# Where VectorE's sums of token chunks stand at the end of a mixture-of-experts stage: among its last three turns, or all behind them

## The chip, the cores and the metric

One core of one Trainium2 chip runs the whole program in one launch. The metric is the device time of that launch in microseconds (us). TensorE (PE), VectorE (DVE), ScalarE (ACT) and GpSimd (POOL) each run their own instruction stream in order; SyncE (SP) does no arithmetic here and issues most of the DMAs. The streams are tied together by semaphores.

## The reference

The input is 16 batches of 256 tokens with 128 features, so 4096 tokens. A causal attention layer with a graph part comes first, then a mixture of experts:

```python
x = x + _L0_attn_ref(_layernorm(x, axis=-1), ...)      # 16 heads of 64, causal
x = x + _L0_ffn_ref(_layernorm(x, axis=-1), ...)
# _L0_ffn_ref: 8 experts, hidden size 352, every token goes to its top 2 experts
normed = _rmsnorm(x, norm_weight)
probs = softmax(normed @ router_weight.T); topk_w, topk_idx = top_k(probs, 2)
for e in range(E):
    hidden = silu(gate) * up
    moe_out = moe_out + combine[..., e, None] * (hidden @ down_weight[e].T)
return x + alpha * moe_out
```

What this study is about is the very last line. Each token's result is its own row plus the two rows that its two experts gave.

## The kernel before

The kernel has a long attention part (one turn for each batch, two batches written out, then a hardware loop) that ends at about 880 us. After it comes the sorted stage. Every token has been copied twice, once for each of its two experts, into a DRAM tensor `slots` in which the copies are sorted by expert and cut into tiles of 128 rows. There are 71 such tiles (`STEPS` = 71), and one step works on one of them:

- SP loads the tile into `zin` (a ring of 8), L436.
- PE transposes it, multiplies it with the expert's gate and up weights (`sorted_gate_up`, L1009), transposes the hidden rows (`hidden_transposed`, L1020) and multiplies them with the down weights into bank 7 (`sorted_down`, L1042).
- ACT takes the high part of the transposed tokens, the silu and the transposed hidden rows out of PSUM. DVE takes the low part (`slots_low`, L1966) and the product of silu and up (`sorted_hidden`, L1971). It then scales the down product out of bank 7 into `zout` (`slots_out`, L1979 to L1984).
- POOL scatters the 128 rows of `zout` into the DRAM tensor `pairs` with an indirect DMA (`rows_out`, L565 to L570). Its landing raises `w_row[j % 8]`.

The steps are software-pipelined. Turn j of DVE's loop runs `sorted_hidden(j)`, `slots_low(j + 2)` and `slots_out(j - 2)`, and the loop has 73 turns (0 to 72). Turn 70 is the last with a `sorted_hidden`; turns 71 and 72 hold only `slots_out(69)` and `slots_out(70)`.

In `pairs` both rows of a token lie side by side. The output is made in 8 chunks of 512 tokens (`CHUNK` = 4 tiles of 128). `fetch(k)` reads chunk k of `pairs` into `got`, 512 KB, and raises `w_got[k]`. Then three rows are added: `x_all`, `got[.., 0, :]` and `got[.., 1, :]`. The chunks are shared out:

- `BY_DVE` = chunks 0, 1, 2 and 6, in two tensor_tensor operations each (`total`, L2019 to L2023). The second one raises `d_sum`.
- `BY_PE` = chunks 3, 4 and 5, by multiplying with the identity and adding up in PSUM (L1112 to L1119), from where ACT copies them back (L1358 to L1361) and raises `a_sum`.
- Chunk 7, `FINAL`, is halved: 256 tokens by DVE, 256 by PE and ACT.

Chunks 0 to 6 hold the batches 0 to 13 and chunk 7 the batches 14 and 15. Rows of the early batches are all out once the first `DONE` steps have landed, so the first seven chunks are fetched before the last steps are through. `FINAL` needs all 71 steps.

SP's stream sets the order of the transfers at the end (L451 to L465). SP works through it in order, and a wait holds everything behind it:

```python
            all_rows(DONE)
            for k in range(CHUNKS_DONE):
                fetch(k)
            for n in range(3):
                store(chunk(BY_DVE[n]), d_sum, n + 1)
            store(chunk(BY_PE[0]), a_sum, 1)
            all_rows(STEPS)
            fetch(FINAL)
            store(chunk(BY_DVE[3]), d_sum, 4)
```

`store(t, by, n)` (L424 to L426) waits until `by` has reached n and then writes 256 KB of `x_all` to the output (128 KB for the halves of chunk 7). `all_rows` (L428 to L430) is eight waits, one for each `w_row`.

Of the kernel before, what the change touches and what calls it, by code (L numbers as in the profile page):

```python
# [36 lines left out]
STEPS = BATCHES * SIDE + EXPERTS - 1  # L37
# [41 lines left out]
def build_program(nc, x, wq, wk, wv, wvT, gnn_w, gnn_b, lin_wT, lin_b, wo, gamma_in, gamma_out,  # L79
# [10 lines left out]
    with ctx:  # L90
# [252 lines left out]
        def live(j):  # L343
            return 0 <= j < STEPS
# [3 lines left out]
            return (j - slot + RING - 1) // RING  # L348

        BY_PE, BY_DVE, FINAL = (3, 4, 5), (0, 1, 2, 6), CHUNKS_OUT - 1  # L350
        AMONG_STEPS = {STEPS - 1: 0, STEPS: 1, STEPS + 1: 2}
        FINAL_PE = slice(FINAL * CHUNK, FINAL * CHUNK + CHUNK // 2)
        FINAL_DVE = slice(FINAL * CHUNK + CHUNK // 2, CHUNKS_OUT * CHUNK)

        def chunk(k):
            return slice(k * CHUNK, (k + 1) * CHUNK)
# [1012 lines left out]
        def _(dve):  # L1369
# [126 lines left out]
            def output_bias(b):  # L1496
                s_og.wait(dve, b, PAIRS)
                V.tensor_scalar(yT[:, :], bank[7][:, 0:TOKENS], yb[:, :], None, ALU.add).then_inc(d_yT.sem, 1)

            def output_kept(b, o):  # L1500
                s_yn.wait(dve, b, 1)
                V.tensor_copy(y_now[:, :, :],  # L1502
                              o.rearrange("p (t d) -> p t d", t=TILES)).then_inc(d_y.sem, 1)
# [462 lines left out]
            def slots_low(j):  # L1966
                a_zh.wait(dve, j, 1)
                V.scalar_tensor_tensor(sz_lo[:, j % 2, :], bank[4][:, 0:P], normw[:, :],
                                       sz_hi[:, j % 2, :].bitcast(f32), ALU.mult, ALU.subtract).then_inc(d_zlo.sem, 1)

            def sorted_hidden(j):  # L1971
                s_gu.wait(dve, 2 * j, 2)
                a_silu.wait(dve, j, 1)
                if j >= 2:
                    s_ht.wait(dve, j - 2, 1)
                V.tensor_tensor(shid[:, j % 2, 0:HID], bank[2 + j % 2][:, 0:HID], ssg[:, j % 2, :],  # L1976
                                ALU.mult).then_inc(d_hid.sem, 1)

            def slots_out(j):  # L1979
                s_down.wait(dve, j, 1)  # L1980
                if j >= RING:
                    dve.wait_ge(w_row[j % RING], 16 * (j // RING))
                V.tensor_scalar(zout[:, j % RING, :], bank[7][:, 0:DIM], zin[:, j % RING, SHARE:SHARE + 1], None,  # L1983
                                ALU.mult).then_inc(d_zout.sem, 1)  # L1984
# [5 lines left out]
            def taken_from_bank(k):  # L1990

                p, last = BATCHES - 2, BATCHES - 1
                if k == 0:
                    take_logits(p, bank[7][:, AUX_LOGITS])
                if k == 4:
                    take_places(p, bank[7][:, AUX_PLACES])
                if k == 19:
                    last_transposed(bank[7][:, AUX_Z])
                if k == 21:
                    take_logits(last, bank[7][:, AUX_LOGITS])  # L2000
                if k == 25:
                    take_places(last, bank[7][:, AUX_PLACES])

            def routed(j):
                p, last = BATCHES - 2, BATCHES - 1
                if 2 <= j < 6:
                    choose(p, (0, 'index', 'hot', 2)[j - 2])
                if 6 <= j < 8:
                    place_tokens(p, j - 6)
                if 8 <= j < 20:  # L2010
                    norm_tokens(last, j - 8)
                if 23 <= j < 27:
                    choose(last, (0, 'index', 'hot', 2)[j - 23])
                if 27 <= j < 29:
                    place_tokens(last, j - 27)
                if 29 <= j < 37:
                    table_rest(j - 29)

            def total(t, k, n):  # L2019
                dve.wait_ge(w_got[k], 16)  # L2020
                V.tensor_tensor(got[:, t, 0, :], got[:, t, 0, :], got[:, t, 1, :], ALU.add).then_inc(d_part, 1)
                dve.wait_ge(d_part, n + 1)
                V.tensor_tensor(x_all[:, t, :], x_all[:, t, :], got[:, t, 0, :], ALU.add).then_inc(d_sum, 1)  # L2023

            def sorted_stage():
                V.memset(shid[:, :, HID:], 0.0)
                slots_low(0)
                output_bias(BATCHES - 1)
                slots_low(1)
                for j in range(STEPS + 2):  # L2030
                    if live(j):
                        sorted_hidden(j)
                    if live(j + 2):
                        slots_low(j + 2)
                    if j == 1:
                        output_kept(BATCHES - 1, bank[7][:, 0:TOKENS])
                    if live(j - 2):
                        s_down.wait(dve, j - 2, 1)
                        taken_from_bank(j - 2)
                        slots_out(j - 2)  # L2040
                    routed(j)
                    if j in AMONG_STEPS:
                        n = AMONG_STEPS[j]
                        total(chunk(BY_DVE[n]), BY_DVE[n], n)

            dve.wait_ge(w_x0, 16)
            norm_step(0, 0)
# [15 lines left out]
            with dve.Fori(2, BATCHES - 1) as b:  # L2063
                batch(b, b - 1, b - 2, b + 1)
            batch(BATCHES - 1, BATCHES - 2, BATCHES - 3, None)
            sorted_stage()
            total(chunk(BY_DVE[3]), BY_DVE[3], 3)
            total(FINAL_DVE, FINAL, len(BY_DVE))


# [22 lines left out]
```

## Time and profile before

| | before |
|---|---|
| median of 3 runs | 1054.04 us (1053.72 to 1056.16) |
| the profiled execution, device time | 1054.87 us |
| its span in the trace | 1053.1 us |
| PE / DVE / ACT / POOL busy | 97% / 81% / 74% / 48% of the span |
| granted TensorE clock, mean | 1.0 |
| got<-pairs, 8 fetches of 512 KB | 6.0 us median from issue to landing |
| out<-x_all, 7 stores of 256 KB | 3.5 us median from issue to landing |

All times in the trace count from the start of the span. The busy shares are means over the whole program; the change touches only the last 17 us. Of DMA issues, "issue" is the moment when the engine hands the transfer over, and "landing" is when the semaphore that it raises is complete.

### The profile page before, as it was taken

Reading aid. Unit: us, or ns where it says so; the run is one execution under the profiler, and the core shown is the slowest. Engines: PE = TensorE matmul, PEld = TensorE weight load, DVE = VectorE, ACT = ScalarE, POOL = GpSimd, SP = SyncE. Lnnn points to the kernel's source line nnn. Section 1 sums busy time; section 2 is a strip of 40 time slices with the busy share of each in tenths; the row PEclk is TensorE's granted clock in tenths of the full one; section 3 lists DMA queues with packets and bytes.
Section 4 is the critical chain, followed back from the end, with each engine's and each line's share of the span. In section 5 each row is a group of like instructions: output and inputs, shape, how many; then the busy total and the mean of one; then the engine's idle time right before and its main releaser. Section 6 shows DMA issues by size and latency. Waiting matters only on the chain.

```text
span 1053.1 us, 27818 instructions
## 1 busy us (share of the span) xinstructions
PE 1022.9 (97%) x8600; PEld 855.3 (81%) x8600; DVE 856.3 (81%) x3622; ACT 777.8 (74%) x2180; POOL 505.3 (48%) x668
## 2 busy tenths in 40 slices
PE   4999999999999999999999999999999999999997
PEld 3888888887888888888887878888887877999995
DVE  4859798989898988889898989898989787767554
ACT  3778787878787878787878787878787785656663
POOL 4524345454545454545454545454545352655443
PEclk9999999999999999999999999999999999999999
DMA  6990000000000000000000000000000022222227
GB/s 176 401 358 15 1 10 12 8 10 8 10 8 10 8 10 8 10 8 10 8 10 8 10 8 10 8 8 11 8 11 5 6 68 54 74 62 72 60 66 249
DMA packets 48965, 50.04 MB, mean 48 GB/s; under 512 B 20601, under 2 KB 39291, under 8 KB 48912
## 3 DMA queue, kind: packets, MB, share of 16 engines
q1 hardware_dynamic: 44592, 40.91, 12.7%
q0 software_dynamic: 4320, 8.47, 2.4%
q8 instruction: 28, 0.46, 0.2%
q14 instruction: 25, 0.20, 0.1%
HBM read 21.23 MB, written 28.58 MB: 47 GB/s over the span
## 4 chain that ended last, share of the span: by engine, by line
PE 78%; DVE 11%; ACT 3%; issue 3%; DMA 2%; SPq 2%; POOL 0%; POOLq 0%; DVEq 0%; ACTq 0%
PE bank L665 65%; DVE eb L1475 4%; DVE ea L1472 3%; PE bank L742 2%; PE bank L752 2%; PE bank L1025 2%; PE bank L753 2%; PE bank L755 2%; DVE nmax L1462 2%; PE bank L777 2%; ACT ea L1159 1%; ACT eb L1159 1%; DMA pairs<-zout,zin 1%; PE bank L1007 1%; DVE y_now L1502 1%
## 5 line engine op out<-in xcount | busy, mean ns | idle before, releaser
L535 POOL TENSOR_TENSOR ea<-ea,wgt 128x256 f32<-128x256 f32 x128 | 79.9, 624 | 273.1 <-DVE wgt L1484 273.0
L1462 DVE TENSOR_REDUCE nmax<-bank 128x1 f32<-128x128 f32 (+1 forms) x512 | 149.7, 347 | 22.3 <-PE bank L665 21.6
L1475 DVE SCALAR_TENSOR_TENSOR eb<-idw,ssum,eb 128x256 f32<-128x256 f32 x256 | 136.9, 570 | 0.0
L537 POOL TENSOR_TENSOR eb<-eb,wgt 128x512 f32<-128x512 f32 x128 | 133.9, 1046 | 0.0
L1159 ACT ACTIVATE eb<-bank,nmax 128x256 f32<-128x256 f32 x256 | 126.8, 495 | 0.0
L1129 ACT ACTIVATE gt<-bank 128x512 f32<-128x512 f32 (+1 forms) x256 | 112.7, 499 | 15.1 <-PE bank L755 12.9
L1159 ACT ACTIVATE ea<-bank,nmax 128x128 f32<-128x128 f32 x256 | 98.4, 385 | 27.1 <-DVE nmax L1462 22.3
L665 PE MATMUL bank<-qk 64*128 64x128 f32 (+1 forms) x1024 | 111.0, 341 | 0.0
L568 POOL DMA_INDIRECT pairs<-zout,zin x71 | 70.8, 997 | 78.7 <-DVE zout L1983 67.2
L665 PE MATMUL bank<-gt,vnat 128*64 128x256 f32 (+1 forms) x1024 | 107.2, 335 | 0.4 <-ACT gt L1129 0.4
L665 PE MATMUL bank<-gt,g 128*64 128x256 f32 (+1 forms) x1024 | 92.2, 327 | 0.3 <-ACT g L1129 0.3
L665 PEld LDWEIGHTS bank<-gt,vnat 128*64 128x64 f32 x1024 | 63.2, 136 | 35.6 <-issue 16.0
L1129 ACT ACTIVATE gvT<-bank 128x256 f32<-128x256 f32 x128 | 49.9, 390 | 55.8 <-DVE aT L1494 55.7
L1472 DVE SCALAR_TENSOR_TENSOR ea<-ident,ssum,ea 128x128 f32<-128x128 f32 x256 | 90.9, 391 | 0.0
L1129 ACT ACTIVATE qk<-bank 128x512 f32<-128x512 f32 x128 | 76.1, 610 | 19.6 <-PE bank L665 18.1
L665 PE MATMUL bank<-xt_lo,w_hi 128*128 128x256 f32 x256 | 87.3, 341 | 2.4 <-DVE xt_lo L1455 1.7
L544 POOL TENSOR_TENSOR deg<-den,rs 128x256 f32<-128x256 f32 x128 | 81.6, 642 | 12.9 <-DVE eb L1475 12.9
L665 PEld LDWEIGHTS bank<-gt,g 128*64 128x64 f32 x1024 | 65.4, 137 | 21.0 <-ACT g L1129 0.7
L665 PE MATMUL bank<-f2T,lwo 128*128 128x256 f32 x256 | 77.7, 386 | 0.3 <-ACT f2T L1192 0.3
L1976 DVE TENSOR_TENSOR shid<-bank,ssg 128x352 f32<-128x352 f32 x71 | 37.2, 524 | 50.1 <-ACT ssg L1322 38.2
L665 PE MATMUL bank<-aT,wo_sb 128*128 128x256 f32 x256 | 73.7, 391 | 0.0
L665 PE MATMUL bank<-xt_hi,w_hi 128*128 128x256 f32 x256 | 72.5, 283 | 0.0
(241 smaller groups left out, 3007.2 us busy)
## 6 DMA issues: line engine op xcount, KB each, us to landing
slots<-gu_lo SPq DMA_DIRECT2D x33, 520.0 KB, 15.0
zin<-slots SPq DMA_DIRECT2D x71, 65.0 KB, 1.9
got<-pairs SPq DMA_DIRECT2D x8, 512.0 KB, 6.0
zin<-in_guT SPq DMA_DIRECT2D x14, 216.0 KB, 2.8
raw_gu<-in_guT SPq DMA_DIRECT2D x8, 352.0 KB, 3.0
out<-x_all SPq DMA_DIRECT2D x7, 256.0 KB, 3.5
pairs<-zout,zin POOLq DMA_INDIRECT x71, 2.3
dn<-in_downT SPq DMA_DIRECT2D x2, 512.0 KB, 15.7
```

What stands on the lines that cost most here:

```text
L535: nc.gpsimd.tensor_tensor(ea[:, s], ea[:, s], wgt[:, s, 0:2].unsqueeze(2).to_broadcast([P, 2, P]), ALU.mult)
L537: nc.gpsimd.tensor_tensor(eb[:, s], eb[:, s], wgt[:, s, 2:4].unsqueeze(2).to_broadcast([P, 2, 2 * P]), ALU.mult).then_inc(p_g.sem, 1)
L544: nc.gpsimd.tensor_tensor(deg[:, s], den[:, s, :].unsqueeze(2).to_broadcast([P, 4, DHEAD]), rs[:, s, :].unsqueeze(2).to_broadcast([P, 4, D ...
L568: nc.gpsimd.indirect_dma_start(pairs, bass.IndirectOffsetOnAxis(ap=zin[:, j % RING, ID:ID + 1].bitcast(u32), axis=0), zout[:, j % RING, :] ...
L665: return nc_mm(o, st, mo, start=first, stop=last, **more)
L742: mm = nc.tensor.transpose(o[:, m * TOKENS + t * P:m * TOKENS + (t + 1) * P], vnat[:, t, n * P:(n + 1) * P], ident[:, :])
L1129: return nc.scalar.activation(o, i, ACT.Copy, **more)
L1159: done = nc.scalar.activation(e[:, s, a, :], score_bank(n, a)[:, TILE_SCORES[t]], ACT.Exp, bias=nmax[:, s, i:i + 1], accum_out=ssum[:, s, ...
L1462: done = V.tensor_reduce(nmax[:, n % 3, i:i + 1], score_bank(n, a)[:, TILE_SCORES[t]], X, ALU.max, negate=True)
L1472: V.scalar_tensor_tensor(ea[:, s, a, :], ident[:, :], ssum[:, s, a:a + 1], ea[:, s, a, :], ALU.mult, ALU.max, accum_out=den[:, s, a:a + 1])
L1475: done = V.scalar_tensor_tensor(eb[:, s, a, :], idw[:, :], ssum[:, s, 2 + a:3 + a], eb[:, s, a, :], ALU.mult, ALU.max, accum_out=den[:, s, ...
L1976: V.tensor_tensor(shid[:, j % 2, 0:HID], bank[2 + j % 2][:, 0:HID], ssg[:, j % 2, :], ALU.mult).then_inc(d_hid.sem, 1)
```

## The change

The three sums that stood in DVE's turns 70, 71 and 72 (behind `slots_out(68)`, `slots_out(69)` and `slots_out(70)`) are taken out of the loop. The four whole chunks are now summed one after the other behind the last turn, in the same order and with the same semaphore counts. Nothing else differs: not SP's stream, not PE's, ACT's or POOL's.

```diff
         BY_PE, BY_DVE, FINAL = (3, 4, 5), (0, 1, 2, 6), CHUNKS_OUT - 1
-        AMONG_STEPS = {STEPS - 1: 0, STEPS: 1, STEPS + 1: 2}
...
                     routed(j)
-                    if j in AMONG_STEPS:
-                        n = AMONG_STEPS[j]
-                        total(chunk(BY_DVE[n]), BY_DVE[n], n)
...
             sorted_stage()
-            total(chunk(BY_DVE[3]), BY_DVE[3], 3)
+            for n, k in enumerate(BY_DVE):
+                total(chunk(k), k, n)
             total(FINAL_DVE, FINAL, len(BY_DVE))
```

## Rows read from the trace of the kernel before

**Rows 1.** Chain that ended last, 1035 to 1054: start us, us, what.
```profile
1035.98 0.36 DVE zout L1983
...
1039.03 1.22 POOL pairs L568
...
1040.96 3.21 DMA pairs<-zout,zin
...
1044.64 4.14 DMA got<-pairs
...
1048.83 1.58 PE bank L665 x6
...
1050.42 0.38 ACT x_all L1129
```

**Rows 2.** Timeline of DVE: start us, us, operation, idle before and its releaser.
```profile
1036.97 0.69 DVE L2023 TENSOR_TENSOR x_all<-x_all,got 128x512 f32<-128x512 f32 x1
1037.91 0.35 DVE L1983 TENSOR_SCALAR zout<-bank,zin 128x128 f32<-128x128 f32 x1 [0.25 <-PE bank L665]
...
1039.83 0.35 DVE L1983 TENSOR_SCALAR zout<-bank,zin 128x128 f32<-128x128 f32 x1 [0.25 <-PE bank L665]
1040.10 0.68 DVE L2021 TENSOR_TENSOR got<-got 128x512 f32<-128x512 f32 x1
1040.82 0.69 DVE L2023 TENSOR_TENSOR x_all<-x_all,got 128x512 f32<-128x512 f32 x1
1041.42 0.68 DVE L2021 TENSOR_TENSOR got<-got 128x512 f32<-128x512 f32 x1
1042.14 0.69 DVE L2023 TENSOR_TENSOR x_all<-x_all,got 128x512 f32<-128x512 f32 x1
1048.80 0.43 DVE L2021 TENSOR_TENSOR got<-got 128x256 f32<-128x256 f32 x1 [5.97 <-DMA got<-pairs]
```

**Rows 3.** Timeline of SP's DMA issues, single ones, same columns.
```profile
1027.93 0.33 SPq L436 DMA_DIRECT2D zin<-slots  x1
...
1028.57 0.33 SPq L422 DMA_DIRECT2D got<-pairs  x1
...
1041.53 0.45 SPq L426 DMA_DIRECT2D out<-x_all  x1
1042.97 0.37 SPq L426 DMA_DIRECT2D out<-x_all  x1
1044.64 0.34 SPq L422 DMA_DIRECT2D got<-pairs  x1
1045.04 0.43 SPq L426 DMA_DIRECT2D out<-x_all  x1
1050.83 0.37 SPq L426 DMA_DIRECT2D out<-x_all  x1
```

**Rows 4.** Timeline of ACT, its first copy of a chunk's sum.
```profile
1042.35 0.60 ACT L1129 ACTIVATE x_all<-bank 128x512 f32<-128x512 f32 x1 [3.68 <-PE bank L665]
```

**Rows 5.** Tile view of x_all on SP, 1042 to 1044: one store, issue to landing.
```profile
L426 SPq DMA_DIRECT2D out<-x_all x1: 372/372/372, 1043.0 to 1043.0; - x1
...
DMA to landing us min/median/max: 2.3/2.3/2.3
```

**Rows 6.** DMA view of 1043 to 1044 in 40 slices, busy tenths.
```profile
DMA  9999999999989999995531111011000000034789
```

**Rows 7.** Tile view of got on SP, seventh fetch alone: issue to landing.
```profile
L422 SPq DMA_DIRECT2D got<-pairs x1: 486/486/486, 1031.5 to 1031.5; - x1
...
DMA to landing us min/median/max: 9.0/9.0/9.0
```

**Rows 8.** Timeline of POOL, scatters of steps 67, 69 and 70.
```profile
1035.03 0.97 POOL L568 DMA_INDIRECT pairs<-zout,zin  x1 [1.01 <-DVE zout L1983]
...
1039.03 1.40 POOL L568 DMA_INDIRECT pairs<-zout,zin  x1 [0.53 <-issue]
1040.96 1.40 POOL L568 DMA_INDIRECT pairs<-zout,zin  x1 [0.53 <-issue]
```

**Rows 9.** Windows of half a microsecond: PE, PEld, DVE, ACT, POOL, clock, DMA share, GB/s.
```profile
1047.50:1048.00 0.50, 0.00 (x0) 0.00 (x0) 0.00 (x0) 0.50 (x1) 0.00 (x0) 1.00 0.97 373
...
1048.50:1049.00 0.50, 0.17 (x1) 0.18 (x2) 0.20 (x1) 0.00 (x0) 0.00 (x0) 1.00 1.15 345
```

## The prediction

> **What bounds the kernel now.** The page says that TensorE is busy for 97% of the span, but the change touches nothing before 1036 us, so that share says nothing about it. I read the chain of work that ended last, and of it only the end [rows 1]. The reader is to see which waits are in it. Up to 1035.98 it is TensorE. Then it goes through DVE's `zout` and POOL's scatters to the last scatter, issued at 1040.96 and landed 3.21 us later, at about 1044.2. From there it goes to SP's fetch of the last chunk at 1044.64, which lands 4.14 us later. PE's last sum (1.58 us), ACT's copy (0.38) and the last store, issued at 1050.83 [rows 3], end the program. None of DVE's sums of whole chunks is in the chain. Two questions are left. Do the sums hold up the `zout`s that are in it? And does the fetch stay where it is when the stores ahead of it on SP come later?
>
> **What the change removes: the sums among the turns.** DVE's timeline answers the first question [rows 2]. The first sum ends at 1036.97 + 0.69 = 1037.66, and the `zout` behind it starts at 1037.91 after 0.25 us of idle time that PE ended. The next one is the same (idle 0.25, ended by PE). So both `zout`s wait for PE's down product and not for a sum; taking the sums away moves neither. Value 0 us. Bounds: no gain above 0, because PE's product is late by itself, and no loss, because nothing is added in front of them.
>
> On POOL the same scatter takes 0.97 us at 1035.03 and 1.40 at 1039.03 and 1040.96 [rows 8]; the 0.43 us come with the sums, as each long one overlaps a second addition of a sum (1040.82 to 1041.51 for the last [rows 2]). After the change the scatters of steps 68 and 69 have no sum beside them and should fall to 0.97. The last one should not: the first sum now starts where the third one did, at 1040.10, right behind the last `zout`, and its second addition again runs from 1040.82 to 1041.51. The last scatter is the one the fetch needs, so 0 us are won.
>
> The Trainium skill's page "SBUF — State Buffer", section "SBUF: two separate sides", says that a VectorE instruction with two SBUF inputs excludes a GpSimd instruction that reads SBUF. The rows above agree (+0.43 us), and by that rule too the last scatter stays at 1.40.
>
> **What it adds: three sums behind the turns.** DVE has four sums to make in a row. From one sum's first addition to the next one's it is 1041.42 - 1040.10 = 1.32 us [rows 2]. The sums then start at 1040.10, 1041.42, 1042.74 and 1044.06, and end 1.41 later (1040.82 + 0.69 - 1040.10): 1041.51, 1042.83, 1044.15 and 1045.47. The fourth one was done at 1042.14 + 0.69 = 1042.83 and is now 2.64 us later. DVE's half of the last chunk starts only at 1048.80 after 5.97 us of idle time [rows 2], which covers that; without this cover it would cost the 2.64.
>
> **What waits for the later sums: SP.** This is the only term that isn't zero. SP issues the three stores of DVE's chunks, PE's first store, eight waits, and then the last fetch, strictly in this order. Before, the third store was issued at 1041.53, PE's first at 1042.97 (released by ACT's copy, 1042.35 + 0.60 [rows 4]), and the fetch at 1044.64 (released by the last scatter) [rows 3]. So SP stood still from 1043.34 until 1044.2, which is cover for a delay. After:
>
> - the third store follows its sum: 1044.15 + 0.02 = 1044.17 (before: 1041.53 after 1041.51)
> - PE's first store has long been ready and follows after one issue of 0.45: 1044.62, and takes 0.37: 1044.99
> - eight waits that are all met: 0.31, from the end of the load before (1027.93 + 0.33 = 1028.26) to 1028.57 [rows 3]
> - the fetch is issued at 1045.30 instead of 1044.64: +0.66 us.
>
> Of 2.64 us of delay about 2.0 are hidden by the time SP stood waiting, first for ACT and then for the last scatter. The last scatter has landed by 1044.2, so its landing no longer sets the fetch; the third sum does.
>
> **What lies in front of the fetch in the DMA engines.** The second cost is unseen in the trace and I bound it. A lone store of 256 KB lands in 2.3 us [rows 5]. The DMA view around it shows the previous store's packets until about 1043.5 and its own from about 1043.9, 0.93 us after its issue at 1042.97 [rows 6]. It was issued 1.44 us after the store before it, whose packets would by the same lag start near 1042.46 and end near 1043.45; so one store keeps the engines busy for an estimated 0.97 us. Before, both stores' packets were through by 1044.9, ahead of the fetch's (1044.64 + 0.93 = 1045.57). After, the third store's packets start at 1045.10 and end at 1046.07, PE's first store's end at 1047.04, and the fetch could start at 1045.30 + 0.93 = 1046.23. If the engines take it in strict order it starts at 1047.04, 0.81 us later still. If its reads overlap with the stores, nothing is added. Lower bound 0, upper bound 0.81. I take 0.4, the middle: a store writes DRAM and a fetch reads it, and no row here has a fetch behind two stores, so neither end is nearer.
>
> The Trainium skill's page "DMA: Bandwidth & Descriptors", section "Queues, rings and completion order", says that descriptors of one queue are consumed in ring order on each DMA engine. No row here tests it; by this rule the cost would be the full 0.81, and the total +1.47 instead of +1.06.
>
> **The sum.** 0.66 + 0.4 = +1.06 us for the landing of the last chunk: 1048.78 becomes about 1049.84. What follows it (PE 1.58, ACT 0.38, the last store) is unchanged: PE's other sums are done at 1047.5 in both. So the span goes from 1053.1 to 1054.2 us. The profiled execution's own time was 1054.87, 1.77 above its span and 0.83 above the median of the runs. On the median the forecast is 1054.04 + 1.06 = 1055.1 us, +0.1%. That is below the 0.3% (3.2 us) that a measurement of this kernel can tell from no change, so the forecast is "no difference", leaning to slower.
>
> **The rivals.**
>
> (a) *The last fetch is caught in a pile of transfers: slower.* In the trace, a fetch landed after 4.14 us when it was nearly alone [rows 1], but the seventh of seven in a row took 9.0 [rows 7]. After the change up to three stores (issued at 1042.85, 1044.17 and 1044.62) are not yet through when the fetch is handed over. If they count like fetches, the fetch takes up to 9.0: +4.86, and with the 0.66 the end is +5.5, 1059.6 us. It decides from a landing of more than 4.14 + 2.5 = 6.6 us on. Against it: the six fetches in front of the seventh were 3 MB, three stores are 0.75 MB. Chance 4%.
>
> (b) *TensorE's clock falls while PE waits for the last chunk.* PE now idles from 1047.5 to about 1049.9 instead of 1048.8. The granted clock is 1.00 in the idle stretch and behind it [rows 9]. If the longer wait brought it to the lower of the two levels (1.2 instead of 2.4 GHz), PE's last sum of 1.58 would take up to twice that: +1.58 on +1.06, 1056.7 us. Nothing in the trace shows such a fall, so 5%, and it too stays within 0.3%.
>
> (c) *The scatters get faster and the fetch earlier: a gain.* The last scatter landed 3.21 us after its issue [rows 1], while the second and third stores of DVE's chunks were under way. If it lost the 0.43 us of contention [rows 8] and SP were ready, the fetch would come at 1044.2: -0.43, 1053.6 us. For this SP would have to be through with the third store by 1043.4, but the third sum ends at 1044.15. Chance 8%, for the case that DVE's four sums run closer together than the 1.32 us read here or that the fetch lands faster behind later stores.
>
> (d) *The change does nothing of what it says.* The order is written out by hand and nothing reorders it, so this has no chance worth a number.
>
> **How the numbers follow.** The forecast (+0.66 to +1.47) has 80%, (a) 4%, (b) 5%, (c) 8%, and 3% are left for something unseen, split over both sides. For 8 in 10 the range runs from the median less (c)'s 0.43 and the spread of the runs' lower side (0.3), 1053.3, up to (b)'s 1056.7 with 0.3 on top, 1057.0; it leaves out (a). By the 0.3% bound: faster 2% (half of the unseen rest), within 93%, slower 5% ((a) and the other half).
>
> **What would show each step.** `zout` at 1037.9 and 1039.8 as before, both still released by PE; the scatters of steps 68 and 69 at 0.97 us and the last at 1.40; four sums in a row, 1.32 apart from 1040.1 on; SP's third store at 1044.2, the fetch at 1045.3; a landing of 4.1 to 5.0 us. In the chain of work, SP's stores and DVE's sums should take the place of the last scatter. The prediction is wrong if the `zout`s come earlier without the sums, if the fetch is issued outside 1045.0 to 1045.6, or if its landing takes over 6.6 us.

## The result and the profile after

| | before | after the change |
|---|---|---|
| median of 22 runs each | 1054.78 us (1053.72 to 1057.39) | 1056.92 us (1055.61 to 1058.45) |
| ratio to before, 95% interval | | 1.0018 (1.0012 to 1.0024) |
| profiled execution: device time, span | 1054.87, 1053.1 us | 1056.03, 1054.3 us |

The change costs 2.1 us by the medians (+0.2%), twice what was forecast. It is clear of zero but within the 0.3% that count as no difference here. The forecast started from a median of 3 runs, 1054.04 us; with 22 runs the kernel before stands at 1054.78.

The two profiled executions differ by only 1.2 us. In the one of after, the last `zout` starts at 1039.06 and not at 1039.83 [rows 2]. This lead is older than the change: the `zout` of step 68, ahead of the first sum that was moved, starts at 1035.21, where it was 1035.98 before [rows 1]. So from here on most times are counted **from the start of the last `zout`**, written +x. Counted so, before ends at 1053.1 - 1039.83 = +13.27 and after at 1054.3 - 1039.06 = +15.24. The difference is 1.97 us, close to the 2.14 of the medians.

The chain of work that ended last, after the change (start us, us, what), against [rows 1]:

```profile
1039.06 0.35 DVE zout L1982
1039.41 0.61 DVE got L2020
...
1042.69 0.70 DVE x_all L2022
1043.40 0.02 issue
1043.41 0.37 SPq L425
1043.79 0.05 issue
1043.84 0.50 SPq L425
1044.34 0.05 issue
1044.38 0.02 SPq L429
...
1044.52 0.03 SPq L429
1044.55 0.35 issue
1044.90 0.03 SPq L429
1044.93 0.05 issue
1044.98 4.37 DMA got<-pairs
...
1049.39 2.25 PE bank L664 x6
...
1051.66 0.38 ACT x_all L1128
```

POOL's scatter, which linked the last `zout` to the fetch before, is gone from the chain. In its place stand three sums of DVE, two stores on SP and SP's waits (the eight waits show as four rows of L429). The row of 0.35 us between two of them is called "issue" in the trace: SP waits for nothing there that the profile shows. It is called a pause below. PE's last sum takes 2.25 us where it took 1.58.

POOL's timeline after, against [rows 8], the scatters of steps 69 and 70:

```profile
1038.26 0.97 POOL L567 DMA_INDIRECT pairs<-zout,zin  x1 [0.95 <-DVE zout L1982]
1040.18 1.40 POOL L567 DMA_INDIRECT pairs<-zout,zin  x1 [0.96 <-DVE zout L1982]
```

The last scatter is still beside a sum, the one ahead of it is free of it. DVE's timeline after has the last `zout`, against [rows 2], still released by PE:

```profile
1039.06 0.35 DVE L1982 TENSOR_SCALAR zout<-bank,zin 128x128 f32<-128x128 f32 x1 [1.57 <-PE bank L664]
```

And windows of half a microsecond (columns as in [rows 9]):

```profile
1049.50:1050.00 0.50, 0.50 (x3) 0.45 (x4) 0.47 (x2) 0.00 (x0) 0.00 (x0) 1.00 1.15 345
1050.00:1050.50 0.50, 0.50 (x3) 0.45 (x2) 0.25 (x1) 0.00 (x0) 0.00 (x0) 0.63 1.07 322
1050.50:1051.00 0.50, 0.50 (x3) 0.34 (x1) 0.00 (x0) 0.00 (x0) 0.00 (x0) 0.50 0.49 147
```

The third column from the right is the granted clock. It goes from 1.00 (2.4 GHz) to 0.50 (1.2 GHz) in the middle of PE's last sum, after PE had nothing to do for 2.71 us. Before, PE idled 1.36 us there and the clock stayed at 1.00 [rows 9].

### The profile page after: what moved, and what is told of

Read it like the earlier page. It is cut to its first block, busy times and chain, and to the rows that moved or that the text cites. A ratio compares the mean times of both kernels' runs of the same rounds, so it can differ in the third digit from the quotient of the medians.

```text
span 1054.3 us, 27818 instructions
## 1 busy us (share of the span) xinstructions
PE 1023.3 (97%) x8600; PEld 855.6 (81%) x8600; DVE 856.2 (81%) x3622; ACT 776.9 (74%) x2180; POOL 503.5 (48%) x668
## 4 chain that ended last, share of the span: by engine, by line
PE 79%; DVE 12%; ACT 3%; issue 3%; SPq 2%; DMA 2%; DVEq 0%; POOLq 0%; ACTq 0%
PE bank L664 65%; DVE eb L1474 4%; DVE ea L1471 3%; PE bank L741 2%; PE bank L751 2%; PE bank L1024 2%; PE bank L754 2%; PE bank L752 2%; DVE nmax L1461 2%; PE bank L776 2%; ACT eb L1158 1%; ACT ea L1158 1%; PE bank L1006 1%; DVE y_now L1501 1%; DVE yT L1497 1%
## 5 line engine op out<-in xcount | busy, mean ns | idle before, releaser
L536 POOL TENSOR_TENSOR eb<-eb,wgt 128x512 f32<-128x512 f32 x128 | 133.6, 1044 | 0.0
```

Source lines behind the costliest of these rows:

```text
L536: nc.gpsimd.tensor_tensor(eb[:, s], eb[:, s], wgt[:, s, 2:4].unsqueeze(2).to_broadcast([P, 2, 2 * P]), ALU.mult).then_inc(p_g.sem, 1)
```

## The experiments

All were run with the kernel before beside them. The values below are from the profiled executions, in us from the last `zout`; the last two columns are from all runs (5 to 22 a kernel). One kernel has one profile, so differences of 0.1 or 0.2 us between two rows of the other columns may be chance. "Lands in" is the time from issue to landing of the last fetch, taken from the chain or, where the fetch isn't in it, from DVE's first work on the chunk.

| run | fetch issued | lands in | PE idle before it | PE's last sum | span ends | median against before | ratio (95%) |
|---|---|---|---|---|---|---|---|
| before | +4.81 | 4.14 | 1.36 | 1.58 | +13.27 | | |
| the change | +5.92 | 4.37 | 2.71 | 2.25 | +15.24 | +2.14 | 1.0018 (1.0012, 1.0024) |
| e1 | +4.77 | 4.44 | 1.63 | 1.58 | +13.50 | +0.38 | 1.0001 (0.9992, 1.0011) |
| e2 | +7.68 | 4.45 | 4.54 | 2.94 | +17.79 | +4.84 | 1.0040 (1.0025, 1.0056) |
| e5 | +7.32 | 4.46 | 4.19 | 2.94 | +17.47 | +3.67 | 1.0034 (1.0024, 1.0044) |
| e4 | +5.92 | 4.38 | none | 1.48 | +15.92 | +2.56 | 1.0025 (1.0014, 1.0037) |
| e4b | +5.92 | 4.54 | 1.16 | 1.58 | +14.74 | +1.47 | 1.0012 (1.0003, 1.0021) |
| e3 | +3.86 | 4.45 | 0.72 | 1.58 | +14.79 | +0.95 | 1.0011 (1.0002, 1.0020) |
| e6 | +3.85 | 4.53 | 0.80 | 1.58 | +14.82 | +1.39 | 1.0013 (1.0004, 1.0022) |
| e7 | +3.43 | 4.54 | 0.39 | 1.58 | +14.43 | +1.23 | 1.0014 (1.0005, 1.0024) |
| e9 | +4.16 | 4.49 | 1.06 | 1.58 | +12.98 | -0.64 | 0.9993 (0.9985, 1.0002) |
| e8 | +4.15 | 4.62 | 1.18 | 1.58 | +13.08 | -0.39 | 0.9994 (0.9986, 1.0003) |
| e10 | +4.15 | 4.42 | 0.98 | 0.95 | +12.78 | -1.17 | 0.9993 (0.9985, 1.0002) |
| e11 | +3.93 | 4.18 | 0.53 | 0.95 | +13.14 | -0.75 | 0.9993 (0.9984, 1.0002) |

### How many sums may move (e1, e2)

e1, from the kernel before:

```diff
-        AMONG_STEPS = {STEPS - 1: 0, STEPS: 1, STEPS + 1: 2}
+        AMONG_STEPS = {STEPS - 1: 0}
...
-            total(chunk(BY_DVE[3]), BY_DVE[3], 3)
+            for n in range(1, 4):
+                total(chunk(BY_DVE[n]), BY_DVE[n], n)
```

> Of the three sums only two leave the turns: the first stays behind the zout of step 68. Times here count from the start of the last zout. Before: the last fetch is issued at +4.81 and ACT's last copy ends at +10.97; after the change +5.92 and +12.98. Theory (SP's order holds the fetch once the third sum ends too late): the third sum ends at +3.00, PE's first store is through at about +3.95 and the eight waits at +4.6, still ahead of the last scatter's landing at about +4.4 to +4.8. So the fetch is issued at +4.8 and the time is that of before, 0 to +0.3 us. Rival (what costs is that stores and sums crowd the end, each sum moved costs its share): one sum less than in the change is moved, so about half of the change's +2, +1.0 us.

The fetch came at +4.77, still set by the last scatter, and the time is that of before. The time alone doesn't exclude the rival's +1.0 us, which lies just inside the interval (1.0011 is +1.2 us); the trace does, as the last scatter still releases the fetch. With only two sums moved nothing is lost that shows; with the third one moved too, its store comes too late.

e2, from the change:

```diff
-            for n, k in enumerate(BY_DVE):
+            for n, k in enumerate((BY_DVE[3],) + BY_DVE[:3]):
                 total(chunk(k), k, n)
...
-                store(chunk(BY_DVE[n]), d_sum, n + 1)
+                store(chunk(BY_DVE[n]), d_sum, n + 2)
...
-            store(chunk(BY_DVE[3]), d_sum, 4)
+            store(chunk(BY_DVE[3]), d_sum, 1)
```

> The change, but chunk 6 is summed first of the four, so that the third store (of chunk 2) waits for the fourth sum. Same work. Theory: the fetch is issued one sum later than after the change, 5.92 + 1.33 = +7.25 us from the last zout; PE waits longer, so its last sum (2.25 us after the change) may take up to 3.2. The time is +1.3 to +2.3 us above the change, +3.3 to +4.3 above before. Rival (crowding): the work at the end is the same as in the change, so the time is that of the change, about +2 above before.

The same sums, and 2.7 us more than the change by the medians. Crowding can't do that; an order on SP can. The time is above what was expected (+3.3 to +4.3): +4.84 by the medians, some +4.2 by the ratio. The fetch is even later than expected (+7.68 for +7.25) because chunk 6's own fetch had not landed: its sum started at +0.69 and not at +0.27.

### What stands in front of the fetch in the DMA engines (e5)

From the change:

```diff
+            sp.wait_ge(d_sum, 3)
             for n in range(3):
                 store(chunk(BY_DVE[n]), d_sum, n + 1)
```

> The change, but SP waits for the third sum before it issues the first store, so four stores of 256 KB go out back to back in front of the fetch. Theory (strict order in the DMA engines, 0.97 us for each store): stores at +4.35, +4.8, +5.2, +5.7 from the last zout, the fetch at +6.8 (0.9 later than in the change); its packets can start only at about +9.2, so it takes 5.5 us to land instead of 4.37. Time +2.0 above the change, +4.0 above before, and a little more if PE's clock falls further. Rival (a fetch overlaps with stores): it lands in 4.1 to 4.4 us, time +0.9 above the change, +2.9 above before.

The landing of 5.5 us did not come. Chain of this run:

```profile
1045.78 0.74 SPq L425
...
1046.65 0.35 issue
1047.01 0.03 SPq L429
...
1047.15 4.46 DMA got<-pairs
...
1051.65 2.94 PE bank L665 x6
```

Four stores went out in 2.32 us, then the fetch, and it lands in 4.46 us, 0.32 more than before. In e3 and e7 (below), with no store in front, it took 4.45 and 4.54; but there stores stand right behind the fetch, so they are no clean zero. Over all runs it took 4.14 to 4.62. So four stores in front cost about 0.3 us at most, and whether even that comes from them is open.

Whose packets run isn't in the views, but their rate is. Quarters of a microsecond (columns as in [rows 9]), of before (first fence, fetch issued at 1044.64) and of e5 (second, fetch issued at 1047.15):

```profile
1045.25:1045.50 0.25, 0.25 (x2) 0.10 (x1) 0.00 (x0) 0.25 (x1) 0.00 (x0) 1.00 0.00 0
1045.50:1045.75 0.25, 0.25 (x2) 0.17 (x1) 0.00 (x0) 0.02 (x1) 0.00 (x0) 1.00 1.60 147
```

```profile
1048.25:1048.50 0.25, 0.00 (x0) 0.00 (x0) 0.00 (x0) 0.00 (x0) 0.00 (x0) 1.00 1.01 299
1048.50:1048.75 0.25, 0.00 (x0) 0.00 (x0) 0.00 (x0) 0.00 (x0) 0.00 (x0) 1.00 0.84 137
```

Before, the fetch's packets begin out of an idle stretch, 0.9 us after its issue, at 147 GB/s. In e5 the rate falls to a like 137 GB/s 1.35 us after the issue. If that is where the stores end and the fetch begins, it began up to 0.5 us later, and the landing shows 0.3 of it. The Trainium skill's page "DMA: Bandwidth & Descriptors", section "Queues, rings and completion order", says that descriptors of one queue are consumed in ring order. The fall from 299 to 137 GB/s would agree with that, and no run here excludes it. What isn't there is the rise to 5.5 us that strict order at 0.97 us a store, the prediction's estimate from rows 5 and 6, would have given. The time was still +3.67, since the fetch was issued 1.4 us later than in the change and PE's last sum ran at 1.2 GHz from its start (granted clock 0.50 from 1051.25 on), taking 2.94 us.

### PE's clock (e4, e4b)

From the change; `range(5)` in e4, `range(2)` in e4b:

```diff
             for n, k in enumerate(BY_PE):
                 total(chunk(k), k, n)
+            for i in range(5):
+                nc.tensor.matmul(bank[4][:, :], ident[:, :], dn[:, 0:4, 0, :], start=True, stop=True)
             total(FINAL_PE, FINAL, len(BY_PE))
```

> The change, with five extra matmuls of 512 columns (results unused) between PE's last whole chunk and its half of the last one, some 2.1 us of PE work inside the 2.7 us it idles. Theory (the granted clock falls after the longer idle time and stretches the last sum): clock 1.00 to the end, the last sum at 1.6 us instead of 2.25, the time 0.6 us under the change, about +1.3 above before. Rival (the drop is only a reading; of the 22 runs of the change the five with a mean clock of 1.0 were not shorter): the last sum stays at 2.2 us and the time at about +2.0.

The extra matmuls took 4.46 us, 0.89 each, because each fp32 matmul is two records in the trace (10 for the five), which the expectation had counted as one. They held PE's last sum by 1.5 us, so the time says nothing; the clock stayed at 1.00.

> The change, with two instead of five extra matmuls on PE between its last whole chunk and its half of the last one. (The five took 4.46 us, 0.89 each, twice what was planned, and held the last sum by 1.5 us; its clock was 1.00 and the sum itself took 1.5.) Two take 1.8 us of the 2.7 that PE idles, so they hold nothing. Theory: clock 1.00 to the end, last sum 1.6 us instead of 2.25, time 0.6 us under the change, +1.3 to +1.5 above before. Rival (the drop is only a reading): last sum 2.2 us, time +2.

PE's timeline, in the change (first fence) and in e4b, where the two matmuls are done before the chunk lands:

```profile
1049.39 1.38 PE L664 MATMUL bank<-got,ident 128*128 128x256 f32 x4 [2.71 <-DMA got<-pairs]
1050.57 1.06 PE L664 MATMUL bank<-x_all,ident 128*128 128x256 f32 x2
```

```profile
1046.83 1.88 PE L1123 MATMUL bank<-dn,ident 128*128 128x512 f32 x4
1049.86 1.13 PE L664 MATMUL bank<-got,ident 128*128 128x256 f32 x4 [1.16 <-DMA got<-pairs]
1050.83 0.59 PE L664 MATMUL bank<-x_all,ident 128*128 128x256 f32 x2
```

The two groups of PE's last sum take 1.38 and 1.06 us in the change, here 1.13 and 0.59. The fetch is issued at +5.92 in both, ACT's last copy ends at +12.48 instead of +12.98, and the median is +1.47 over before instead of +2.14. The intervals of the two ratios overlap, so the 0.5 us rests on the two profiles. e2 and e5 go the same way: after 4.54 and 4.19 us without work the sum takes 2.94 us.

The mean clock of a run, which is known for all of them, settles nothing, because it also counts what comes after PE's last sum. In e10 that sum ended at 1049.08, and the clock (third column from the right) fell only behind it:

```profile
1051.00:1052.00 1.00, 0.00 (x0) 0.00 (x0) 0.00 (x0) 0.00 (x0) 0.00 (x0) 0.98 0.17 48
1052.00:1053.00 1.00, 0.00 (x0) 0.00 (x0) 0.00 (x0) 0.00 (x0) 0.00 (x0) 0.50 0.00 0
```

It was below 1.0 in 17 of 22 runs of the change, 2 of 11 of e4b and all 14 of e2 and e5, but also in 8 of 27 of before beside e1 and in 9 of 11 of e6, whose profile has PE idle for only 0.80 us. In the change the five runs at 1.0 have a median of 1056.70 us and the other 17 of 1057.23; their times overlap. How often the clock falls within the last sum is not known.

### SP's order instead of DVE's (e3, e6)

e3 from the change, e6 from before, with the same edit:

```diff
+            all_rows(STEPS)
+            fetch(FINAL)
             for n in range(3):
                 store(chunk(BY_DVE[n]), d_sum, n + 1)
             store(chunk(BY_PE[0]), a_sum, 1)
-            all_rows(STEPS)
-            fetch(FINAL)
```

> The change, but SP waits for the last rows and issues the last fetch ahead of the first four stores. Theory (SP's order is what makes the later sums cost): the fetch is issued at +4.8 us from the last zout as before, though all four sums still stand behind the turns; it lands at +9.0 to +9.3, PE's last sum takes 1.6 at clock 1.00, ACT's last copy ends at about +11.0. The six stores that now follow the fetch may hold the last stores by up to 0.6. Time 0 to +0.6 us above before, so 1.4 to 2 of the change's +2 come back. Rival (the sums' place costs by itself, by crowding or by DVE's later end): the time stays at +1.5 to +2.

> The kernel before, with SP's order of the run above: sums among the turns, last fetch ahead of the stores. Theory: with the fetch freed from the sums their place is worth nothing, so this run and the one above are the same within 0.3 us; the fetch is issued at +4.8 (set by the last scatter's landing) and nothing is won over before: 0 to +0.6. Rival (sums' place costs by itself): this run is 1.5 to 2 us faster than the one above.

With the fetch in front, the sums' place is worth nothing that shows: 1.0011 and 1.0013, spans ending at +14.79 and +14.82. The end alone would prove little, since the stores set it now (below); but the fetch's issue (+3.86 and +3.85) and the end of ACT's last copy (+10.34 and +10.40) don't depend on the sums' place either. So it is through SP's order that the change costs. But both are slower than before, by more than expected, although the fetch is issued 0.95 us earlier. Windows of e3 (its fetched chunk landed at 1047.62, ACT's last copy ended at 1049.65):

```profile
1050.00:1051.00 1.00, 0.00 (x0) 0.00 (x0) 0.00 (x0) 0.00 (x0) 0.00 (x0) 1.00 1.15 346
1051.00:1052.00 1.00, 0.00 (x0) 0.00 (x0) 0.00 (x0) 0.00 (x0) 0.00 (x0) 1.00 1.14 342
1052.00:1053.00 1.00, 0.00 (x0) 0.00 (x0) 0.00 (x0) 0.00 (x0) 0.00 (x0) 1.00 0.73 218
```

No engine works any more, and the DMA engines are still full (last two columns: busy share, GB/s) until the window from 1052 on, where it is 0.73. Seven whole stores stand behind the fetch (the expectations say six, and three instead of four for e9), where before it is three, and the last store, which lands 1.8 us after its issue at 1050.83 in the kernel before [rows 3], takes 3.4. SP itself falls behind too. This is its last issue in e3:

```profile
1050.32 0.85 SPq L425 DMA_DIRECT2D out<-x_all  x1
```

It takes 0.85 us instead of 0.37 and starts 0.67 us after the copy that it waits for, because the issues in front of it took up to 1.20. The bound has moved from the fetch to the draining of the output.

The fetch at +3.86 shows one thing more. The last scatter landed in 2.57 us here, in 3.21 before [rows 1] and in 3.17 in e1. e9 tells why: there only the third store was moved behind the fetch, and the scatter landed in 2.56. So a store issued at about +1.7, beside the scatter, holds up its landing by 0.6 us.

### The sum beside the scatter (e7)

From e3:

```diff
+            dve.wait_ge(s_sum, 1)
             for n, k in enumerate(BY_DVE):
                 total(chunk(k), k, n)
```

> As the run with the change and the fetch first, and DVE's sums wait besides until PE's first sum is done (about +2.5 us from the last zout), so that none is beside the last scatter (+1.1 to +2.5). Theory A (the addition with two SBUF operands stretches the scatter, and the stretch delays its landing): the last scatter takes 0.97 us instead of 1.40, the last fetch is issued at +4.4 instead of +4.8, the time is 0.4 us under the run with the fetch first. Theory B (only the instruction's end is shown later, or the landing is set by the DMA engines): scatter 0.97, fetch still at +4.8, no gain.

Chains of e3 (first fence) and e7 (second):

```profile
1040.43 2.57 DMA pairs<-zout,zin
...
1043.17 4.45 DMA got<-pairs
```

```profile
1041.60 2.14 DMA pairs<-zout,zin
...
1043.90 4.54 DMA got<-pairs
```

Scatter 0.97 us, landing 0.43 us earlier, fetch at +3.43 for +3.86: the 0.43 us of theory A. The time did not follow (+1.23 against +0.95 by medians, the intervals overlap), because in this order the stores set the end. So the additions with two SBUF operands do delay a scatter beside them. By how much depends on where they fall: in e2, where the first addition starts later (+0.69), the last scatter takes 1.10 us. The Trainium skill's page "SBUF — State Buffer", section "SBUF: two separate sides", has this as an exclusion against GpSimd instructions that read SBUF; the trace agrees, and in this pair of runs the 0.43 us reach the transfer's landing.

### Towards a version that beats both (e9, e8, e10, e11)

e9, from before: the third store goes behind the fetch.

```diff
-            for n in range(3):
+            for n in range(2):
                 store(chunk(BY_DVE[n]), d_sum, n + 1)
             store(chunk(BY_PE[0]), a_sum, 1)
             all_rows(STEPS)
             fetch(FINAL)
+            store(chunk(BY_DVE[2]), d_sum, 3)
```

> The kernel before with one move on SP: only the first two stores and PE's first stay ahead of the last fetch, the third store (chunk 2) goes behind it. The fetch lands after it is issued as in all runs so far (4.1 to 4.5 us). With stores in flight the last scatter took 3.2 us to land, with none 2.57. Theory (a store under way holds up the scatter's landing, and the fetch with it): the last scatter lands in about 2.6 to 2.9 us and the fetch is issued at +4.0 to +4.4 instead of +4.8, time 0.3 to 0.8 us under before, since the stores behind the fetch are fewer (3 whole ones) than the pile that ate the gain when all stores stood behind it. Rival (any store moved behind the fetch delays the last stores by as much): no gain, 0 to +0.3.

e8 adds, in DVE's `total` behind the wait for `d_part`:

```diff
+                if n == 2:
+                    dve.wait_ge(s_sum, 1)
```

> The run above, and the third sum's second addition waits for PE's first sum (+2.5 us), so that it is not beside the last scatter. Theory: scatter 0.97 instead of 1.40 us, fetch another 0.43 us earlier, at +3.6 to +4.0, time 0.7 to 1.2 us under before. Rival: the stores that end later (third at +3.2 instead of +1.7) give it back at the end, no gain over the run above.

e10 sets the split of the last chunk to `FINAL * CHUNK + CHUNK // 4` in both slices.

> The run above, with the last chunk split one tile to PE and three to DVE instead of two and two. PE's part with ACT's copy took 1.6 + 0.4 us, DVE's 0.9. Three tiles on DVE take about 1.15 us (between 0.9 for two and 1.4 for four), one tile on PE with the copy about 1.1. Theory: the last store is issued 0.8 us earlier and, with 192 KB instead of 128, takes 2.0 instead of 1.8: time another 0.6 us under the run above, about 1.5 under before. Rival (the stores ahead in the DMA engines end last by now): no gain.

e11 also puts `store(chunk(BY_PE[0]), a_sum, 1)` behind the fetch.

> The run above with PE's first store behind the last fetch too. In it the fetch was issued at +4.15 us from the last zout, set by PE's first store (+3.13) and the eight waits, not by the scatter any more. Theory: now the undisturbed scatter sets it again, fetch at +3.4 to +3.5 as in the run with an undisturbed scatter and no store in front; but five whole stores and the fetch then stand in line in the DMA engines, which were busy to +13.4 with six behind the fetch and would be to about +12.4 with five, where the run above ends at +12.8 in all. So the 0.7 us won at the fetch are lost at the end: the same time as the run above, -0.3 to +0.5. Rival (the fetch's issue sets the end): 0.7 us faster than the run above, about 1.5 under before.

In e9 the fetch comes at +4.16 and the span ends 0.3 us earlier than before. In e8 the scatter falls to 0.97 us as meant, but the fetch stays at +4.15: PE's first store, issued at about +3.1, and the eight waits with their pause now set it. That expectation (+3.6 to +4.0) was wrong. In e10 the last copy of ACT ends at +9.86 instead of +10.79, but the end moves by only 0.3, not 0.6. In e11 the last scatter sets the fetch again, but it lands in 2.65 us and not in the 2.14 of e7, though it too takes 0.97 on POOL. So the fetch comes 0.2 us earlier, not 0.7. In e11 two stores stand ahead of the scatter, in e7 none; whether they hold it was not tried. The end is 0.4 us later, and the last two stores take 2.7 to 3.0 us to land, in e10 2.1 to 2.2: the draining takes over, as its theory said. All four measure 0.9993 or 0.9994 with intervals that include 1. They point to 0.4 to 1.2 us less than before, but that one of them is faster than before is not shown; that all are faster than the change is (their intervals end below 1.0012, where its own begins).

## Why the prediction was right, and where it was not

**The time: inside the range by very little.** The range was 1053.3 to 1057.0, and the median after is 1056.92. The rise is 2.14 us for a forecast of 1.06, on a base that turned out 0.74 us too low. "No difference" held because 0.3% is 3.2 us, wide enough to hide two missing terms; that is more luck than working. And one of the prediction's own signs of being wrong came true: the fetch was to be issued between 1045.0 and 1045.6. It was issued at 1044.98, and counted from the `zout` of before at 1039.83 + 5.92 = 1045.75, which is outside too.

**The bound: right.** DVE's sums are not in the chain of before, and whether the fetch stays where it is was the right question.

**The `zout`s and scatters: right.** The last `zout`s are 1.93 us apart (before 1.92) and wait for PE; the scatter of step 69 fell to 0.97 us and the last stayed at 1.40. That the last one could be won back was shown only in e7.

**DVE's four sums: right.** The third sum was forecast to end 4.32 us after the last `zout` (1044.15 - 1039.83) and ended at 4.32 (1042.69 + 0.69 - 1039.06). e1 confirms the slack: one sum less behind the turns, and the fetch is back at +4.77.

**SP's way to the fetch: the right mechanism, a term too small.** The forecast was +0.66 us, the trace shows +1.11 (+5.92 against +4.81). The step that failed is "eight waits that are all met: 0.31". That was read at another place of SP's stream, ahead of the first fetch. At this place the waits contain a pause of 0.35 us and take 0.64 (1044.34 to 1044.98), and PE's store takes 0.50 instead of 0.37. The chain of before has the same pause, between the scatter's landing and the fetch, and the prediction passed over it:

```profile
1044.18 0.03 SPq L430
1044.21 0.35 issue
1044.57 0.03 SPq L430
```

It is in e1, e2 and e4b too, at the same wait.

**The landing behind stores: inside its bounds, the middle too large.** Forecast +0.4 (0 to 0.81), measured +0.23. Where the 0.23 come from is open: e1, with SP's order of before and the fetch at nearly the same place, has +0.30, and e3, with no store in front, +0.31. Rival (a) is dead: not even four stores in a pile took the landing near 6.6 us.

**PE's last sum: wrong.** "What follows it is unchanged" is the step that failed. The sum took 2.25 us instead of 1.58, +0.67, by rival (b)'s mechanism, which had been given 5%: the granted clock went to 0.50, and with PE kept at work (e4b) the sum was back at 1.58. The argument against it was that no fall is seen in the trace of before; but a trace with 1.36 us of idle time says nothing about 2.7. Its price was too high (+1.58), since the clock fell only in the middle of the sum.

The terms of the profiles add up: 1.11 + 0.23 + 0.67 = 2.01, and ACT's last copy ends at +12.98 instead of +10.97. The point forecast of +1.06 was half of it. SP's way to the fetch was sized 0.45 too small and PE's clock, put at nothing, was worth 0.67; the landing, 0.17 too large, made up a little.

## What to carry to other kernels

Work that is moved off an engine's own critical path still moves what is queued behind its result on another engine's in-order stream: count the slack there, with the cost of each wait and issue read at that very place, not at another one. When PE waits longer for its last piece of work, price that work at the lower clock too. And an earlier critical transfer is worth only as much as the bytes that it pushes behind itself allow: e3 issued the fetch 0.95 us earlier than before, and its span ended 1.5 us later.

## What the runs showed of the hardware that was not expected

- SP pauses 0.35 us at one place of its stream among waits that are met, in before and in the change alike. With one wait added ahead (e5) the pause comes one wait earlier, with a store and its wait moved from ahead to behind (e9) it comes directly in front of the fetch. So in these runs it keeps to a position in the stream, not to an event. What makes it was not tried.
- DVE additions with two SBUF operands beside an indirect DMA on POOL lengthen it from 0.97 to 1.40 us (1.10 in e2), and its landing comes 0.43 us later (e3 against e7).
- A 256 KB store to DRAM that is issued beside the last scatter delays its landing by 0.6 us (3.17 and 3.21 with it in e1 and before, 2.56 and 2.57 without in e9 and e3), while four such stores in front of a 512 KB fetch (e5, 4.46 us) add about 0.3 us at most to it (4.14 before, 4.14 to 4.62 in all runs).
- With many stores queued behind the fetch, one issue on SP takes up to 1.20 us instead of 0.37 (e3).
- PE's granted clock fell to 0.50 within the last sum after 2.71 us without work in the profiled execution of the change, and had fallen before the sum began after 4.19 and 4.54 us (e5, e2). It stayed at 1.00 through the last sum in the profiled executions with 1.63 us or less.
